# A two-layer cross-attention kernel: order of the opening's work and loads, the wait places of the weights, and filler matmuls on an idle TensorE

## The chip, the cores and the metric

The kernel runs on one core of a Trainium2 chip. The metric is the device time of one execution in microseconds (us), lower is better. Before the change the median of three runs is 1741.35 us (1740.72 to 1744.32).

## The reference

Two layers of grouped-query cross-attention are applied one after the other to `x` (32 batches, 112 rows, 512 features). The context (32 x 375 x 512) and an additive mask (32 x 112 x 375, all zeros in these inputs, but read and honoured) are the same for both layers; each layer has its own weights. Everything is float32. Per layer:

```
q = x @ Wq + bq           # 32 heads of 16, in 8 groups of 4
k = ctx @ Wk + bk         # 8 key heads of 16
v = ctx @ Wv + bv
scores = q . k / 4 + mask                     # 32 batches, 32 heads, 112 x 375
out = softmax(scores) @ v                     # over the 375
x = layernorm(out @ Wo + bo + x) * gamma + beta
```

## The kernel before

**Units and slots.** A unit is one batch of one layer. Units have a parity p (0 or 1) and a number n, batch 2n+p of layer 0 for n below PER = 16, of layer 1 above. The program is a row of slots (p, i), i from -1 to 33, p = 0 and then 1 in each i. Every engine runs its own program over the same slots, and they meet by semaphores alone. In slot (p, i) (function `units`) the work of several units lies side by side: the scores, exponentials and first half of the weighted values of the main unit (p, i); the row maxima and the values' projection of the unit ahead (1-p, i+p); the second half of weighted values and the first output heads of the unit behind; the projection of keys of unit (p, i+1) and, in slots of parity 0, of the queries of both parities; the last heads, the residual and the layer norm of the unit stored. A slot has 12 pieces; tables (`STEPS_AT`, `KEYS_AT`, `VALUES_AT`, `QUERIES_AT`, `COLUMNS_AT`, ...) say which work goes into which piece. `table_row(p, i)` picks the row: 0 or 1 by parity, and 2 for the slot (1, -1).

**Exact scores on bfloat16.** Queries and keys are split into three bfloat16 parts each (ScalarE casts and GpSimd subtracts), and small DMAs stack six products of parts along the contraction, 12 DMAs for each half of the heads of a unit: `stack_terms` on SyncE's queue (SP), `send` on ScalarE's (ACT) in the opening. The row maxima come first: 14 steps a unit, in each of which TensorE fills a pair of PSUM banks (L1090) and VectorE reduces it (L922); the step n+2 waits until the reduce n is done. Once a half's maxima are done, GpSimd splits them (L603 to L609), TensorE turns them (`max_columns`, L1122), ScalarE copies them (`mT`, L759), and one DMA (`max_rows`, L411) puts them as three more rows under the queries of the main unit. `scores` waits for it at pieces 0 and 6. The exponentials (L740) then need no more subtraction.

**The opening.** SyncE issues, in this order: Wk, context (0,0), Wq, the queries' input of both parities, context (1,0), Wv, and five of seven parts of the mask's bits. ScalarE's queue has issued the other two parts of the bits before anything else (`BEARLY = 2`). VectorE reduces each part of the bits to a column (L898) and all to one flag (L900 to L904); from it TensorE picks a program with or without the mask's addition. Ahead of that, TensorE runs the projections of slots (0, -1) and (1, -1): keys (0,0), the queries, keys (1,0), values (0,0). After the flag, slot (1, -1) has only the maxima of unit (0,0), and then (0, 0) starts, the first full slot.

**Weights.** In the opening slot (1, -1) SyncE issues `max_rows(0, 0, 1)` after the keys' stack, and then Wo and the rows bo, gamma, beta of layer 0. `next_layer`, called at the end of SyncE's slot, issues layer 1's Wk, bk, Wv, bv and three rows at (0, 0), half of Wq at (1, 0), the rest at (0, 1), half of Wo at (1, 1), the rest at (0, 14). TensorE, VectorE and GpSimd wait for all of layer 0's (`w_in[0]`) at the start of slot (1, 0), and for all 12 of layer 1's (`w_in[1]`) at the start of (0, 15). SyncE's queue is in program order: what is issued late for one unit makes all behind it late.

Of the kernel before, what the change touches and what calls it, by code (L numbers as in the profile page):

```python
# [15 lines left out]
NG = NH // NKV  # L16
LAYERS = 2
PAR = 2
# [29 lines left out]

BEARLY = 2
# [20 lines left out]


LATE_HEADS_AT = [{}, {0: (2,), 1: (3,)}]
HEADS_AT = [{10: (0,), 11: (1,)}, {8: (0,), 9: (1,), 10: (2,), 11: (3,)}]
KEYS_AT = [{2: (0,), 3: (1, 2), 4: (3,)}, {2: (0, 1), 3: (2, 3)}, {0: (0, 1, 2, 3)}]
VALUES_AT = [{1: (0, 1), 2: (2,)}, {4: (0,), 5: (1,), 6: (2,)}, {0: (0, 1, 2)}]
# [5 lines left out]
QUERY_PARTS_AT = [7, 5, 1]  # L81
QUERY_REST_AT = [9, 6, 2]
SEND_QUERIES_AT = 3
# [5 lines left out]
OUT_AT = [(11, 1), (9, 1)]  # L89
KEYS_END = [max(at) for at in KEYS_AT]  # L90
# [3 lines left out]
def step_order(q):  # L94

    order, whole, n = [], 0, 0
    for k in range(PIECES):
        first = min(STEPS_AT[q][k], (k not in WORK_FIRST[q]) + (k in WORK_LAST[q]))
        here = []
        for part, count in ((0, first), (1, k in MIXED_AT[q]), (2, STEPS_AT[q][k] - first)):  # L100
            for _ in range(count):
                half, tiles = (0 if k == 0 else 1, (MIXED, MIXED + TILES // 2)) if part == 1 else \
# [9 lines left out]
ORDER = [step_order(q) for q in range(PAR + 1)]  # L112
# [33 lines left out]
def table_row(p, i):  # L146

    return 2 if first_values(p, i) else p
# [7 lines left out]
def first_outputs(p, i):  # L156

    return isinstance(i, int) and (p, i) == (1, 0)
# [28 lines left out]
def cross_attention_two_layers(nc, xT_d, x_d, ctxT_d, mask_d, mflat_d, W, out):  # L187
# [4 lines left out]
    with ExitStack() as ctx:  # L192
# [96 lines left out]
        w_in = two(sem, "w_in")  # L289
        mf_in = [sem(f"mf_in{n}") for n in range(BLOADS)]  # L290
# [53 lines left out]
        NK, NQ, NV, NW = 2, 2, 2, (4, 12)  # L344
# [4 lines left out]
        def _(sp):  # L349
# [105 lines left out]
            def slot(p, i, has, lay):  # L455
# [28 lines left out]
                if m_ok:  # L484
                    load_x(p, main, lay[0])
                if j_ok:
# [17 lines left out]
                if isinstance(i, int):  # L504
                    next_layer(p, i)
# [26 lines left out]
            ROWS = [(bo, "bo"), (gamma, "gamma"), (beta, "beta")]  # L532

            def load_rows(L, landed):
                for dst, key in ROWS:
                    load_row(dst, L, key, landed)

            def next_layer(p, i):

                if (p, i) == (0, 0):  # L540
                    load_wk(1, w_in[1])
                    load_wv(1, w_in[1])
                    load_rows(1, w_in[1])
                if (p, i) == (1, 0):
                    load_wq(1, w_in[1], slice(0, 2))
                if (p, i) == (0, 1):
                    load_wq(1, w_in[1], slice(2, DC))
                if (p, i) == (1, 1):
                    load_wo(1, w_in[1], slice(0, 2))
                if (p, i) == (0, PER - 2):  # L550
                    load_wo(1, w_in[1], slice(2, NG))
# [6 lines left out]
            load_ctx(1, 0, 0)  # L558
            load_wv(0, w_v)
            for n in range(BEARLY, BLOADS):  # L560
# [8 lines left out]
        def _(pool):  # L569
# [5 lines left out]
            nc.gpsimd.memset(ks[1][:, :, :], 1.0).then_inc(ids, 1)  # L575
            nc.gpsimd.memset(vs[1][:, :, :, :, 1], 1.0).then_inc(ids, 1)
            pool.wait_ge(ids, 7)
# [7 lines left out]
            nc.gpsimd.memset(neghalf[:, :], -0.5).then_inc(ones_set, 1)  # L585

            def slot(p, i, has, lay):
# [4 lines left out]
                if first_outputs(p, i):  # L592
                    pool.wait_ge(w_in[0], 16 * NW[0])
# [32 lines left out]
                def key_parts():  # L626
                    pool.wait_ge(k_p1[p], proj + 1)
                    nc.gpsimd.tensor_tensor(kr[:, :], kf[:, :], kp[p][:, 0, :], ALU.subtract).then_inc(k_r[p], 1)  # L628
                    pool.wait_ge(k_p2[p], proj + 1)
                    nc.gpsimd.tensor_tensor(kp[p][:, 2, :], kr[:, :], kp[p][:, 1, :], ALU.subtract).then_inc(k_p3[p], 1)  # L630

# [18 lines left out]
                def residual_rows():  # L650
                    pool.wait_ge(x_in[o], 16 * (post + 1))
# [24 lines left out]
                elif first_values(p, i):  # L676
                    key_parts()
                    query_rests()
                    query_parts()
                    max_parts(o, 0, ahead, None)  # L680
                elif p == 0:
# [38 lines left out]
        def _(act):  # L720
            def slot(p, i, has, lay):
# [85 lines left out]
                if opens(p, i) and p == 0:  # L807
# [32 lines left out]
                for k in range(PIECES):  # L840
# [31 lines left out]
                    if opens(p, i) and k == SEND_QUERIES_AT:  # L872
                        act.wait_ge(q_p1[p], 2)
                        act.wait_ge(q_p2[p], 2)
                        act.wait_ge(q_p3[p], 2)
                        send(0, qs[p], qp, 0, range(PARTS))
# [10 lines left out]
        def _(dve):  # L887
# [18 lines left out]
            def slot(p, i, has, lay):  # L906
# [4 lines left out]
                if first_values(p, i):  # L911
                    dve.wait_ge(w_v, 16 * NV)
                if first_outputs(p, i):
                    dve.wait_ge(w_in[0], 16 * NW[0])
# [9 lines left out]
                def values():  # L924
                    dve.wait_ge(v_ps[o], ahead + 1)
# [31 lines left out]
                def centred():  # L957
# [381 lines left out]
```

## Time and profile before

| | |
|---|---|
| median of three runs | 1741.35 us |
| the profiled execution | 1738.81 us |
| its span, first to last instruction | 1737.0 us |
| TensorE busy | 1695.1 us, 98% |
| VectorE, ScalarE, GpSimd busy | 73%, 60%, 33% |
| mean granted TensorE clock | 0.99 |

PE is TensorE's matmul, PEld its weight load, DVE VectorE, ACT ScalarE, POOL GpSimd, SPq and ACTq the issue of DMAs on SyncE's and ScalarE's queues. Times are us from the first instruction. A clock of 1.00 is 2.4 GHz and 0.50 is 1.2 GHz; a window that has both shows a mean. Ahead of the first clock record of an execution the view shows 1.00 whatever the clock was. A float32 matmul of the program is two instructions in the trace. Sizes in KB are of 1024 bytes. In the view of sums a row has the window in us, its length, the busy us and the count of instructions (x) of PE, PEld, DVE, ACT and POOL, the mean granted clock, the DMA engines' share and GB/s. In the views in time order a row has start, us, engine, line, operation, operands and count, and in brackets the idle time before it and what ended it.

### The profile page before, as it was taken

The numbers are of one execution on the slowest core, as the hardware profiler recorded it, in microseconds if no ns is written. First come the engines' busy times: TensorE is split into PE (matmuls) and PEld (weight loads), VectorE is DVE, ScalarE is ACT, GpSimd is POOL, SyncE is SP. The second block draws the span as 40 slices with busy tenths as digits, with TensorE's granted clock in tenths as the row PEclk, the third lists the DMA queues.
The fourth block names the chain that finished last, engine by engine and source line by source line (L and its number), as shares of the span: only waits on it lengthen the run. The fifth ranks groups of instructions, "written<-read, shape, count | busy, mean of one in ns | idle before, by whom it ended". The sixth has DMA issues, their size and how long they took to land. (4 is left out here: it accounts for less than half of the span.)

```text
span 1737.0 us, 35992 instructions
## 1 busy us (share of the span) xinstructions
PE 1695.1 (98%) x10881; PEld 1005.9 (58%) x10881; DVE 1267.2 (73%) x1713; ACT 1042.3 (60%) x2370; POOL 572.3 (33%) x1169
## 2 busy tenths in 40 slices
PE   5999999999999999999999999999999999999997
PEld 3555566665565665565665565655665655656652
DVE  5567777787777777777777776777767877767776
ACT  2556666666665656665656665666656666656564
POOL 3133332333332333332333323333323333323332
PEclk8899999999999999999999999999999999999999
DMA  8546555455545465555565454455454455453541
GB/s 283 146 121 170 147 122 143 128 145 143 147 120 142 124 151 145 135 130 147 128 156 145 114 136 130 118 135 145 105 135 125 128 138 139 109 135 115 139 113 55
DMA packets 288390, 235.83 MB, mean 136 GB/s; under 512 B 140858, under 2 KB 262964, under 8 KB 288084
## 3 DMA queue, kind: packets, MB, share of 16 engines
q1 hardware_dynamic: 266852, 204.14, 43.8%
q10 hardware_dynamic: 21488, 31.06, 7.3%
q8 instruction: 27, 0.44, 0.1%
q14 instruction: 23, 0.19, 0.0%
HBM read 101.39 MB, written 22.02 MB: 71 GB/s over the span
## 5 line engine op out<-in xcount | busy, mean ns | idle before, releaser
L922 DVE TENSOR_REDUCE mx<-ms 128x2 f32<-128x750 f32 x896 | 809.2, 924 | 399.0 <-PE ms L1090 392.5
L740 ACT ACTIVATE probs<-sc 125x448 f32<-125x448 f32 x1522 | 744.6, 542 | 281.8 <-PE sc L1061 274.7
L1090 PE MATMUL ms<-ks,qs 96*128 96x375 bf16 (+1 forms) x2560 | 443.0, 327 | 11.4 <-DVE mx L922 8.7
L1061 PE MATMUL sc<-qs,ks 99*125 99x448 bf16 x1522 | 429.2, 358 | 6.0 <-DMA qs<-mT 3.7
L1111 PE MATMUL pv<-probs,vs 125*32 125x448 f32 x3048 | 313.2, 544 | 0.0
L1061 PEld LDWEIGHTS sc<-qs,ks 99*125 99x125 bf16 x1522 | 192.7, 137 | 204.2 <-ACT probs L740 127.8
L1090 PEld LDWEIGHTS ms<-ks,qs 96*128 96x128 bf16 (+1 forms) x2560 | 174.8, 98 | 194.3 <-issue 66.2
L1165 PE MATMUL job<-wo,on 128*112 128x512 f32 x504 | 258.2, 594 | 0.0
L936 DVE RECIPROCAL orec<-osum 128x112 f32<-128x112 f32 x256 | 213.0, 834 | 6.8 <-DMA osum<-oraw 6.8
L1183 PE MATMUL job<-xT,wq 128*128 128x224 f32 x1008 | 214.5, 356 | 0.0
L1134 PEld LDWEIGHTS job<-wv,ctxT 128*125 128x125 f32 x1536 | 191.5, 189 | 16.5 <-issue 0.3
L1148 PE MATMUL pv<-ctxT,wk 128*128 128x375 f32 x512 | 190.1, 484 | 10.7 <-DMA ctxT<-in_ctxT 10.7
L1183 PEld LDWEIGHTS job<-xT,wq 128*128 128x128 f32 x1008 | 187.4, 190 | 19.6 <-ACT qf L782 7.3
L1134 PE MATMUL job<-wv,ctxT 128*125 128x128 f32 x1536 | 196.0, 274 | 0.0
L1111 PEld LDWEIGHTS pv<-probs,vs 125*32 125x32 f32 x3048 | 86.1, 109 | 179.3 <-issue 171.7
L748 ACT COPY oraw<-pv 128x448 f32<-128x448 f32 x127 | 67.6, 532 | 200.1 <-PE pv L1111 200.1
L628 POOL TENSOR_TENSOR kr<-kf,kp 128x375 f32<-128x375 f32 x64 | 57.3, 895 | 357.7 <-ACT kp L771 357.7
L648 POOL TENSOR_TENSOR rstd<-veps,neghalf 112x1 f32<-112x1 f32 x64 | 36.4, 569 | 258.1 <-DVE veps L955 258.1
L1148 PEld LDWEIGHTS pv<-ctxT,wk 128*128 128x128 f32 x512 | 93.4, 192 | 47.0 <-issue 12.8
L617 POOL TENSOR_TENSOR on<-oc,orec 128x224 f32<-128x224 f32 x126 | 83.4, 662 | 86.3 <-DVE orec L936 85.7
L603 POOL TENSOR_TENSOR mwide<-mx,zero 128x14 bf16<-128x14 f32 x128 | 27.3, 213 | 241.9 <-DVE mx L922 234.5
L636 POOL TENSOR_TENSOR qr<-qf,qp 128x224 f32<-128x224 f32 x128 | 75.7, 613 | 69.0 <-ACT qp L796 69.0
(70 smaller groups left out, 1034.5 us busy)
## 6 DMA issues: line engine op xcount, KB each, us to landing
ctxT<-in_ctxT SPq DMA_DIRECT2D x64, 750.0 KB, 4.7
qs<-qp SPq DMA_DIRECT2D x756, 56.0 KB, 2.5
ks<-kp SPq DMA_DIRECT2D x765, 46.9 KB, 2.7
osum<-oraw ACTq DMA_DIRECT2D x125, 112.0 KB, 2.9
oc<-oraw ACTq DMA_DIRECT2D x125, 112.0 KB, 3.6
mask<-in_mask SPq DMA_DIRECT2D x64, 164.1 KB, 5.1
xT<-in_xT SPq DMA_DIRECT2D x32, 224.0 KB, 4.6
xin<-in_x SPq DMA_DIRECT2D x32, 224.0 KB, 3.0
```

Source lines behind the costliest of these rows:

```text
L617: nc.gpsimd.tensor_tensor(on[:, cols], oc[:, cols], orec[:, cols], ALU.mult).then_inc(on_ready[o], 1)
L636: nc.gpsimd.tensor_tensor(qr[:, cols], qf[:, p, cols], qp[:, 0, cols], ALU.subtract)\
L740: nc.scalar.activation(probs[0:KCS, k, j, :], bank[0:KCS, 0:GL], ACT.Exp)\
L922: nc.vector.tensor_reduce(mx[o][:, cols], ms[n % 2][:, :, 0:S2], AX_X, ALU.max).then_inc(max_done[o], 1)
L936: nc.vector.reciprocal(orec[:, S * n:S * n + S], osum[:, S * n:S * n + S])\
L1061: last = nc.tensor.matmul(bank[0:KCS, 0:GL], ks[p][0:KM, g, rows], qs[p][0:KM, g, :], start=True, stop=not masked)
L1090: last = nc.tensor.matmul(to, qs[o][0:KT, group, cols], ks[o][0:KT, group, :], start=True, stop=not masked)
L1111: last = nc.tensor.matmul(bank[32 * j:32 * j + 32, 0:GL], vs[u][:, chunk, 4 * h + j, :, :].rearrange("s d two -> s (d two)"), probs[0:KCS, ...
L1134: last = nc.tensor.matmul(job[0:KCS, P * c:P * c + P], ctxT[o][:, t, KCS * c:KCS * c + KCS], wv[lay[1]][:, t, :], start=(t == 0), stop=(t ...
L1148: last = nc.tensor.matmul(pv[:, 0:S2], wk[lay[3]][:, t, :], ctxT[p][:, t, :], start=(t == 0), stop=(t == DC - 1))
L1165: last = nc.tensor.matmul(bank[0:S, 0:D], weighted[:, S * c:S * c + S], wo[layer][:, c, :], start=(c == 0), stop=(c == NG - 1))
L1183: last = nc.tensor.matmul(bank[:, PAR * S * (c % 2):PAR * S * (c % 2 + 1)], wq[lay[3]][:, t, c, :], xT[:, t, :, :].rearrange("p u l -> p ( ...
```

## The change

It does five things. The mask's bits go all on SyncE's queue, ahead of context (1,0) and Wv, which now are issued inside the opening slot (0, -1), among the stacking DMAs. TensorE no longer runs slot (1, -1)'s projections ahead of the flag: keys (1,0) go into pieces 0 to 3 and values (0,0) into pieces 8 to 10 of slot (1, -1), after the flag, beside the maxima. Slot (0, 0) gets a table row of its own (row 3), with no maxima in pieces 0 and 1. TensorE runs 3 filler matmuls (float32, 112 x 448) before the keys and 12 between the queries and the flag. The loads of layer 0's Wo, bo, gamma, beta and of layer 1's weights are spread to the middle of slots, after `load_x`, and each wait for them is moved to the instruction that uses them. GpSimd's preparation of `ident` no longer waits for two memsets.

```diff
+CLOCK = (3, 12)
-KEYS_AT = [..., {0: (0, 1, 2, 3)}]
-VALUES_AT = [..., {0: (0, 1, 2)}]
+KEYS_AT = [..., {0: (0,), 1: (1,), 2: (2,), 3: (3,)}]
+VALUES_AT = [..., {8: (0,), 9: (1,), 10: (2,)}]
-QUERY_PARTS_AT = [7, 5, 1]
-QUERY_REST_AT = [9, 6, 2]
-SEND_QUERIES_AT = 3
+QUERY_PARTS_AT = [7, 5, 0]
+QUERY_REST_AT = [9, 6, 1]
+SEND_QUERIES_AT = (7, 7)
+for table in (STEPS_AT, KEYS_AT, VALUES_AT, COLUMNS_AT, MIXED_AT, QUERY_PARTS_AT, QUERY_REST_AT, WORK_FIRST, WORK_LAST):
+    table.append(table[0])
+STEPS_AT[3] = [0, 0, 2, 2, 1, 2, 1, 1, 0, 2, 0, 1]
+MIXED_AT[3] = (2, 8)
+KEYS_AT[3] = {3: (0,), 4: (1, 2), 5: (3,)}
...
+        NK, NQ, NV, NW, NR = 2, 2, 2, (3, 7), (2, 5)
...
             def opening_slot(p):
+                if p == 1:
+                    max_rows(0, 0, 1)
                 sp.wait_ge(k_p3[p], 1)
                 if p == 0:
                     stack_terms(0, 0, ks[0], kp[0], 1)
+                    stack_terms(0, 1, ks[0], kp[0], 1, of=(1, 2))
                     sp.wait_ge(q_p1[0], 2)
                     stack_terms(0, 0, qs[0], qp, 0, of=(0,))
-                    stack_terms(0, 1, ks[0], kp[0], 1, of=(1, 2))
+                    stack_terms(0, 1, ks[0], kp[0], 1, of=(0,))
+                    load_ctx(1, 0, 0)
+                    load_wv(0, w_v)
                     stack_terms(0, 1, qs[0], qp, 0, of=(0,))
                     load_mask(0, 0, 0)
                 else:
                     stack_terms(1, 0, ks[1], kp[1], 1)
                     load_ctx(0, 1, 0)
                     for u in range(PAR):
                         load_xT(u, 1, 0)
-                    max_rows(0, 0, 1)
-                    load_wo(0, w_in[0])
-                    load_rows(0, w_in[0])
+                    load_wo(0, w_in[0], slice(0, 2))
...
                 if m_ok:
                     load_x(p, main, lay[0])
+                if isinstance(i, int):
+                    weights(p, i)
                 if j_ok:
                     sp.wait_ge(k_p3[p], keys)
...
-                if isinstance(i, int):
-                    next_layer(p, i)
...
+            def weights(p, i):
+                if (p, i) == (0, 0):
+                    load_wo(0, w_in[0], slice(2, NG))
+                    load_row(bo, 0, "bo", w_in[0])
+                if (p, i) == (1, 0):
+                    load_row(gamma, 0, "gamma", rows_in[0])
+                    load_row(beta, 0, "beta", rows_in[0])
+                if (p, i) == (0, 1):
                     load_wk(1, w_in[1])
                     load_wv(1, w_in[1])
-                    load_rows(1, w_in[1])
-                if (p, i) == (1, 0):
+                if (p, i) == (1, 1):
                     load_wq(1, w_in[1], slice(0, 2))
-                if (p, i) == (0, 1):
+                if (p, i) == (0, PER - 2):
                     load_wq(1, w_in[1], slice(2, DC))
-                if (p, i) == (1, 1):
-                    load_wo(1, w_in[1], slice(0, 2))
-                if (p, i) == (0, PER - 2):
-                    load_wo(1, w_in[1], slice(2, NG))
+                if (p, i) == (1, PER - 2):
+                    load_wo(1, rows_in[1], slice(0, 2))
+                if (p, i) == (0, PER - 1):
+                    load_wo(1, rows_in[1], slice(2, NG))
+                if (p, i) == (1, PER - 1):
+                    for dst, key in ((bo, "bo"), (gamma, "gamma"), (beta, "beta")):
+                        load_row(dst, 1, key, rows_in[1])
             load_wk(0, w_k)
             load_ctx(0, 0, 0)
             load_wq(0, w_q)
             load_xT(0, 0, 0)
             load_xT(1, 0, 0)
-            load_ctx(1, 0, 0)
-            load_wv(0, w_v)
-            for n in range(BEARLY, BLOADS):
+            for n in range(BLOADS):
                 sp.dma_start(mbits[:, BROW * n:BROW * (n + 1)], mbits_d[n]).then_inc(mf_in[n], 16)
...
                 elif first_values(p, i):          # GpSimd, slot (1, -1)
-                    key_parts()
                     query_rests()
                     query_parts()
+                    key_rests()
                     max_parts(o, 0, ahead, None)
+                    key_lasts()
...
-                    act.wait_ge(k_p3[0], 1)       # ScalarE, slot (0, -1)
-                    act.wait_ge(ones_set, PAR)
-                    send(1, ks[0], kp[0], 1, (0,))
...
-            for n in range(BEARLY):
-                act.dma_start(mbits[:, BROW * n:BROW * (n + 1)], mbits_d[n]).then_inc(mf_in[n], 16)
...
+            def keep_clock(times):
+                for _ in range(times):
+                    nc.tensor.matmul(ms[0][0:S, 0, 0:GL], ident4[:, 0, :], ident4[:, :, :].rearrange("p c l -> p (c l)"),
+                                     start=True, stop=True)
+            keep_clock(CLOCK[0])
             pe.wait_ge(w_k, 16 * NK)
-            for p in range(PAR):
-                slots(False, opening=True)(p, -1, exists(p, -1), layers(p, -1))
-            pe.wait_ge(idd, 3)
+            slots(False)(*FIRST, exists(*FIRST), layers(*FIRST))
+            keep_clock(CLOCK[1])
             pe.wait_ge(flag_col, BLOADS + 1)
```

## Rows read from the trace of the kernel before

**Rows 1.** The page, part 1: busy us, share of the span, instructions.
```profile
PE 1695.1 (98%) x10881; PEld 1005.9 (58%) x10881; DVE 1267.2 (73%) x1713; ACT 1042.3 (60%) x2370; POOL 572.3 (33%) x1169
```
**Rows 2.** Waits of TensorE, whole span: us in total, times, longest us.
```profile
PE pv L1148 <- DMA ctxT<-in_ctxT: 10.7, 1, 10.7
...
PE sc L1061 <- DMA qs<-mT: 3.7, 1, 3.7
```
**Rows 3.** Sums, one slot's first exponential to the next's: (0,0), (1,0), (1,1), (0,3), (1,3).
```profile
47.41:76.07 28.66, 27.86 (x163) 18.63 (x165) 13.83 (x16) 16.46 (x38) 5.95 (x15) 0.89 0.35 105
76.07:107.07 31.00, 26.22 (x155) 13.96 (x144) 16.41 (x19) 15.55 (x36) 8.21 (x18) 0.89 0.58 164
134.87:159.65 24.78, 24.78 (x158) 13.06 (x157) 19.22 (x27) 15.70 (x35) 8.61 (x18) 1.00 0.66 170
212.38:240.31 27.93, 27.75 (x184) 18.20 (x184) 20.42 (x27) 16.96 (x39) 9.06 (x19) 1.00 0.45 126
240.31:264.88 24.57, 24.57 (x159) 13.15 (x159) 19.25 (x27) 15.52 (x35) 8.60 (x18) 1.00 0.71 164
```
**Rows 4.** TensorE in time order, 231 to 242 us, in slot (0, 3).
```profile
232.71 2.46 PE L1111 MATMUL pv<-probs,vs 125*32 125x448 f32 x24
...
237.25 1.02 PE L1165 MATMUL job<-wo,on 128*112 128x512 f32 x2
238.11 0.63 PE L1061 MATMUL sc<-qs,ks 99*125 99x448 bf16 x2
```
**Rows 5.** SyncE's queue in time order, slot (1, 0) and the like slot (1, 1).
```profile
75.73 0.42 SPq L515 DMA_DIRECT2D wk<-in_Wk  x1
...
79.11 0.62 SPq L365 DMA_DIRECT2D mask<-in_mask  x1
...
90.06 0.78 SPq L411 DMA_DIRECT2D qs<-mT  x1
...
135.58 1.81 SPq L365 DMA_DIRECT2D mask<-in_mask  x1
...
145.05 0.76 SPq L411 DMA_DIRECT2D qs<-mT  x1
```
**Rows 6.** TensorE and VectorE in time order, the opening.
```profile
10.65 5.34 PE L1148 MATMUL pv<-ctxT,wk 128*128 128x375 f32 x8 [10.65 <-DMA ctxT<-in_ctxT]
15.79 3.38 PE L1183 MATMUL job<-xT,wq 128*128 128x224 f32 x16
22.04 2.69 PE L1148 MATMUL pv<-ctxT,wk 128*128 128x375 f32 x8
24.57 2.78 PE L1134 MATMUL job<-wv,ctxT 128*125 128x128 f32 x24
29.36 1.72 DVE L898 TENSOR_REDUCE mcols<-probs 128x1 f32<-128x1500 uint32 x1 [2.16 <-DMA probs<-in_mask_bits]
31.41 0.37 PE L1261 MATMUL sc<-ident,mcol 128*1 128x128 f32 x1 [4.07 <-DVE mcol L900]
33.64 1.56 PE L1090 MATMUL ms<-ks,qs 96*128 96x375 bf16 x10 [1.85 <-DMA qs<-qp]
35.88 11.05 DVE L922 TENSOR_REDUCE mx<-ms 128x2 f32<-128x750 f32 x12
```
**Rows 7.** Sums of the opening's stretches, columns as in rows 3.
```profile
0.00:10.65 10.65, 0.00 (x0) 0.03 (x1) 3.96 (x5) 1.49 (x2) 5.19 (x15) 1.00 0.75 282
27.35:33.64 6.29, 0.37 (x1) 0.08 (x2) 2.30 (x4) 1.58 (x3) 1.79 (x2) 0.70 1.10 187
33.64:46.80 13.16, 11.03 (x42) 2.24 (x42) 11.92 (x14) 1.67 (x5) 3.15 (x8) 0.50 0.61 166
```
**Rows 8.** DMA issues over the span: count, KB each, median us to landing.
```profile
ctxT<-in_ctxT SPq DMA_DIRECT2D x64, 750.0 KB, 4.7
probs<-in_mask_bits ACTq DMA_DIRECT2D x2, 750.0 KB, 7.0
wk<-in_Wk SPq DMA_DIRECT2D x2, 256.0 KB, 4.7
```

More of the change, by code:

```diff
@@ L47 @@
 BLOADS = 7
-BEARLY = 2
 BROW = B * S * S2 // (BLOADS * P)
@@ L101, in step_order @@
             for _ in range(count):
-                half, tiles = (0 if k == 0 else 1, (MIXED, MIXED + TILES // 2)) if part == 1 else \
+                half, tiles = (MIXED_AT[q].index(k), (MIXED, MIXED + TILES // 2)) if part == 1 else \
                     (whole // len(WHOLE), WHOLE[whole % len(WHOLE)])
@@ L109, in step_order @@
     return order
-ORDER = [step_order(q) for q in range(PAR + 1)]
+ORDER = [step_order(q) for q in range(len(STEPS_AT))]
 OPENS = [[min(n for at in o for n, h, _, _ in at if h == half) for half in range(2)] for o in ORDER]
@@ L146, in table_row @@
 def table_row(p, i):
-    return 2 if first_values(p, i) else p
+    return 2 if first_values(p, i) else 3 if isinstance(i, int) and (p, i) == (0, 0) else p
 def opens(p, i):
@@ L156, in first_outputs, with first_rows @@
 def first_outputs(p, i):
-    return isinstance(i, int) and (p, i) == (1, 0)
+    return isinstance(i, int) and (p, i) in ((1, 0), (1, PER))
+def first_rows(p, i):
+    return isinstance(i, int) and (p, i) == (0, 1)
 def last_scores(p, i):
@@ L289, in cross_attention_two_layers @@
         w_in = two(sem, "w_in")
+        rows_in = two(sem, "rows_in")
         mf_in = [sem(f"mf_in{n}") for n in range(BLOADS)]
@@ L650, in residual_rows @@
                 def residual_rows():
+                    if first_outputs(p, i) and i == 0:
+                        pool.wait_ge(w_in[0], 16 * NW[0])
+                    if first_outputs(p, i) and i == PER:
+                        pool.wait_ge(rows_in[1], 16 * NR[1])
                     pool.wait_ge(x_in[o], 16 * (post + 1))
@@ L676, in slot @@
                 elif first_values(p, i):
-                    key_parts()
                     query_rests()
                     query_parts()
+                    key_rests()
                     max_parts(o, 0, ahead, None)
+                    key_lasts()
                 elif p == 0:
@@ L871, in slot @@
                             cast_rests(h)
-                    if opens(p, i) and k == SEND_QUERIES_AT:
+                    if opens(p, i) and k == SEND_QUERIES_AT[0]:
                         act.wait_ge(q_p1[p], 2)
+                        send(0, qs[p], qp, 0, (0,))
+                    if opens(p, i) and k == SEND_QUERIES_AT[1]:
                         act.wait_ge(q_p2[p], 2)
                         act.wait_ge(q_p3[p], 2)
-                        send(0, qs[p], qp, 0, range(PARTS))
-            for n in range(BEARLY):
-                act.dma_start(mbits[:, BROW * n:BROW * (n + 1)], mbits_d[n]).then_inc(mf_in[n], 16)
+                        send(0, qs[p], qp, 0, (1, 2))
             act.wait_ge(warm_set, 1)
@@ L1016, in slot @@
                             reciprocal(k - RECIPROCALS_AT[p])
+                if first_outputs(p, i) and i == PER:
+                    dve.wait_ge(rows_in[1], 16 * NR[1])
             run(dve, slot)
@@ L1022, in _, with slots @@
         def _(pe):
-            def slots(masked, opening=False):
+            def slots(masked):
                 def slot(p, i, has, lay):
@@ L1037, in slot @@
                     job_free = [(o_evac[p], stored + 1) if s_ok else (mt_evac[p], 2 * main + 1) if m_ok else None]
-                    if first_values(p, i):
-                        job_free[0] = (q_evac, NG // 2) if opening else (v_ready[o], 1)
+                    if isinstance(i, int) and (p, i) == (0, 0):
+                        job_free[0] = (v_ready[p], 1)
                     def take_job_bank():
@@ L1129, in project_values @@
                             take_job_bank()
-                        if first_values(p, i):
+                        if 0 in chunks and first_values(p, i):
                             pe.wait_ge(w_v, 16 * NV)
@@ L1163, in project_outputs @@
                             pe.wait_ge(on_ready[u], 2 * n + heads[0] // 2 + 1)
+                        if 0 in heads:
+                            if first_outputs(p, i) and i == 0:
+                                pe.wait_ge(w_in[0], 16 * NW[0])
+                            if first_outputs(p, i) and i == PER:
+                                pe.wait_ge(rows_in[1], 16 * NR[1])
                         for c in heads:
@@ L1217, in maxima @@
                         def maxima(part):
-                            for n, half, tiles, place in ORDER[q][k] if a_ok and not opening else ():
+                            for n, half, tiles, place in ORDER[q][k] if a_ok else ():
                                 if place == part:
                                     maximum(n, half, tiles, place)
-                        if k == 0 and a_ok and masked and not opening:
+                        if k == 0 and a_ok and masked:
                             pe.wait_ge(mask_in[o], 16 * (ahead + 1))
-                        if k == PIECES - 1 and a_ok and not masked and not opening:
+                        if k == PIECES - 1 and a_ok and not masked:
                             pe.wait_ge(mask_in[o], 16 * (ahead + 1))
@@ L1246, in slot @@
                             maxima(1)
-                        if k == COLUMNS_AT[q][0] and a_ok and not opening:
+                        if k == COLUMNS_AT[q][0] and a_ok:
                             max_columns(o, 0, ahead)
```

45 lines of the change are left out of this document (17 added, 28 removed).

## Prediction

> **What bounds the kernel.** I read the page's busy shares first: TensorE is busy for 98% of the span [rows 1], and no other engine comes above 73%. So only three things can move the time: TensorE's idle time, stretches at the low clock, and the work given to it. The list of TensorE's waits says where it idles. Two of its large entries are single waits: 10.7 us for the first context, and 3.7 us for a row of maxima [rows 2]. The sums by slot say where else time goes. In the steady state a pair of slots takes 27.93 + 24.57 = 52.50 us at clock 1.00. The first pair takes 28.66 + 31.00 = 59.66 us at a mean clock of 0.89 in both [rows 3], although it has less to do.
>
> How much less: slot (0, 0) has no unit behind it, so it lacks one half of weighted values (24 instructions, 2.46 us) and two output heads, each 0.86 us from its start to the start of what follows; slot (1, 0) lacks two heads [rows 4]. That is 2.5 + 1.7 + 1.7 = 5.9 us. The first pair's warm need is 52.5 - 5.9 = 46.6 us, and it has 59.66 - 46.6 = 13.1 us too much. Of these the clock explains (1 - 0.89) x 59.66 = 6.6 us (at half clock two us do the work of one, and the mean clock is the share of work done), the wait for the row of maxima 3.7 us, and the rest, 2.8 us, is smaller waits and idle time of slot (1, 0), where TensorE was busy for 26.22 of 31.00 us.
>
> **The change part by part.**
>
> *Loads spread, waits where they are used.* In slot (1, 0) SyncE begins with seven loads of layer 1 between 75.73 and 79.11 us, then issues the mask, 12 stacking DMAs and the row of maxima at 90.06. That row is what scores wait for at piece 6. From mask to row it takes 10.95 us there, and 9.47 us in slot (1, 1) [rows 5]. So the row is late by 3.4 us of issue and 1.5 us of slower issue behind full queues, together 4.9 us, which is more than the wait of 3.7 us. The change takes all seven loads out of this place. What is put into slot (1, 0) instead, gamma and beta, comes behind the row and `load_x`. The wait goes. What is late next is TensorE's own work, as in slot (1, 3), which is 24.57 us busy of 24.57. The low clock behind the wait goes with it. In slot (0, 0) SyncE gets half of Wo and bo ahead of the next keys' stack: two issues, about 1 us, beside TensorE's full work; if its cover is gone it costs that 1 us. In slot (0, 1) four loads, in (1, 1) one, and two, one, one and three around the layers' border come at the same place. Parity 1 has the tighter queue (9.47 us of issue without a pause), so its three row loads in (1, 15), some 1.3 us, could show; slot (1, 1) took 24.78 us with loads beside it, 0.21 above (1, 3) [rows 3]. I take 0 for all of them, between -0.5 and +2. The moved waits themselves guard loads issued a slot or more ahead: 0. In the case that one holds, what is queued behind it is TensorE's output heads, and the norm behind them.
>
> *Slot (0, 0)'s low clock.* TensorE ran the opening slot at 0.50 [rows 7], because it had nothing in it but maxima in step with VectorE's reduces (12 reduces in 11.05 us, 0.92 each [rows 6]), and took this clock into slot (0, 0). After the change the opening slot holds the dense projections of keys and values, so I expect the clock high at its end. Gain in the pair by both parts: 13.1 us. Against it stands the new table row of slot (0, 0): no maxima in pieces 0 and 1, then three steps in piece 2. VectorE needs 0.92 us for each, TensorE less, so it waits for one or two reduces: 1 us (0 to 2). The pair then takes 47.6 us: **-12.1 us**.
>
> *The flag.* Its last part of the bits is read at 29.36 us, and TensorE has the column at 31.41 [rows 6]. Ahead of this part before stood context (1,0) (750 KB) and Wv with its row (256 + 62 KB, Wv as large as Wk) [rows 8], 1.09 MB, which now come later. The loads ran at 282 GB/s up to 10.65 us and near 400 later; at 0.4 MB/us that is 2.7 us. The flag's matmul comes at 28.7 us. The bounds are 0 (the stacking DMAs of ScalarE's queue, now 4 us earlier, share the engines with the last bits) and -4.
>
> *The first context.* 2 x 750 KB of bits were issued ahead of everything on ScalarE's queue and shared the engines with it. Without them it lands sooner, by 0 to 4 us (1.54 MB at 0.4 MB/us); I take 2.5 us, so keys start at 8.2 us.
>
> *Filler matmuls.* The trace has none. The nearest row is the keys' float32 matmul of 375 columns: 8 instructions in 5.34 us at first, 2.69 us later [rows 6]. For 448 columns that is 0.40 us an instruction at the fast pace and 0.80 us at the slow. Three fillers are 6 instructions, 2.4 to 4.8 us, and are over before 8.2 us if `ident4` is ready by 3.4 us, which GpSimd's shorter preparation allows (its 15 instructions took 5.19 us before [rows 7]). Cost 0; they may save up to 2.7 us of the keys. The queries' input was there by 15.79 at the latest; 2.5 us sooner is 13.3, and 32 instructions (15.79 to 22.04, 6.25 us) end at 19 to 19.6 us. The 12 fillers, 24 instructions, then take 9.6 us, to about 29 us. That is level with the flag at 28.7: cost 0 to 0.5 us. At the slow pace they would take 19.2 us (a rival below).
>
> *The opening slot.* From flag to first maxima 2.23 us passed, and a queries' stack ended that wait [rows 6]; now 28.9 + 2.2 = 31.1 us. Before, the slot took 13.16 us, set by VectorE [rows 7]. Now keys (1,0) stand in piece 0 behind two maxima, and wait for context (1,0). Its issue is behind 12 stacking DMAs, and its data behind the bits. About 18 such DMAs of 50 KB (0.9 MB) at 187 GB/s, the rate of 27.35 to 33.64 us [rows 7], take 4.8 us from the last bits at 26.6, and then 0.77 MB at 0.4 MB/us 1.9 us: 33.3 us. All later maxima are queued behind this wait on TensorE, so VectorE, GpSimd's split and the row of maxima are late by it: about 1.4 us, between 0 and 4. Values (0,0) in pieces 8 to 10 are 24 instructions in 2.78 us, 0.93 a chunk [rows 6], and a step of maxima costs TensorE 11.03 / 14 = 0.79 us at half clock, so 0.4 to 0.5 at full. Such a piece has 1.4 us of TensorE against 0.92 of VectorE: 3 x 0.5 = 1.5 us. The keys' chunks, 0.67 us, hide. Slot: 13.2 + 1.4 + 1.5 = 16.1 us, end at 47.2 us against 46.8: **+0.4 us**, between -4 and +5. So the opening gives nothing for itself: what the flag wins is spent on projections that before ran in the shadow of the wait for it.
>
> *Removed from ScalarE and GpSimd.* Three stacking DMAs change queue and `key_lasts` comes later; both lie beside VectorE's maxima: 0.
>
> **Sum.** -12.1 + 0.4 = -11.7 us. From the profiled execution's 1738.81 us (span 1737.0 and 1.8 around it) this makes 1727.1 us. The median of the three runs is 2.54 us above the profiled one, so the forecast for the median is 1729.6 us.
>
> **A rule weighed against it.** The opening slot's row shows clock 0.50 for a TensorE that is busy for 11.03 of 13.16 us [rows 7]; it had idled 5.9 us of the 6.3 us before. The Trainium skill, "TensorE: Matmul & The Clock Gate", in "HAM oscillation — how this bites in real kernels", says that waits for DMAs between bursts of matmuls bring the array back to its low clock, burst after burst. By it fillers that end 2 us ahead of the maxima, and a wait for a context right behind those, leave the slot low again, and the time would be that of the first rival, 1734; by the row alone, which has a longer pause, it stays open. The trace agrees as far as the fall goes: it shows it behind two pauses, of 4.07 and of 3.73 us.
>
> **Rivals.**
> (a) *The clock falls in the opening slot, and returns with the dense pieces.* For: pauses of 2.2 and 1.4 us follow each other with little between them, and both pauses of 4 us in this trace were followed by 0.50. Against: they are shorter. Price: keys and the maxima among them at half clock, 4 chunks x 0.67 and 4 pairs x 0.3 us, some 3.9 us, and half a us more later: 1729.6 + 4.4 = 1734.
> (b) *The moved loads keep part of the wait.* For: no pause in parity 1's queue. Against: slot (1, 1) had loads and took only 24.78 us. Price: the 3.7 us stall shrinks to half, and smaller ones of 1 us come in (0, 1), (1, 1) and (1, 15), 1.9 + 2 = 3.9 us: 1733.5.
> (c) *The opening wins too.* If the context (1,0) is there in time and bits land 4 us sooner, the slot's end moves from 47.2 to 43.2: 1725.6.
> (d) *Slower: the long fillers run at the slow pace.* If the clock isn't up when they start, they take 19.2 us, the queries 12.5 and the keys 5.3: 8.2 + 5.3 + 12.5 + 19.2 = 45.2 us, and the flag's matmul waits for them, 16.3 us behind the forecast's 28.9. 1729.6 + 16.3 = 1745.9. It decides from the point where the fillers end over 28.9 + 11.7 = 40.6 us. Against it: the queries and second keys ran at the fast pace 5 us behind the first keys [rows 6].
> (e) *The change doesn't do what it says:* the pair's excess has another cause, say DMA traffic of the contexts, and stays: 1740 to 1742.
>
> **How the numbers follow.** Chances: forecast 0.52, (a) 0.17, (b) 0.10, (c) 0.14, (d) 0.04, (e) 0.03. The forecast's own range is 1727 to 1733. For 8 in 10 it has to reach towards (a) and (c), and takes in the opening's bounds of -4 and +4: 1724.5 to 1736. A measurement of this kernel can't tell less than 0.2%, 3.5 us, from no change, so faster means below 1737.9 and slower above 1744.8. (d) is slower; (e) and a tenth of (a) and (b) are within: faster 0.90, same 0.06, slower 0.04.
>
> **What would show it.** The slot sums: first pair at 47 to 49 us from its first exponential to that of (0, 1), clock 1.00. TensorE's waits: none for qs<-mT at L1061, and a new one of 1 to 2 us for the context at L1148 in slot (1, -1). The first exponential at 46 to 49 us. Keys' first 8 instructions under 4 us. Steady pairs at 52.4 to 52.6 us as before. The forecast is wrong if the clock is 0.50 beyond 40 us, if the flag's matmul comes right behind a filler well after 29 us, or if the pair still takes over 52 us.

## The result and the profile after

The changed kernel takes 1729.24 us (median of 4 runs, 1728.31 to 1732.09) against 1741.77 for the kernel before (4 runs): ratio 0.9929, 95% interval 0.9911 to 0.9946. The forecast was 1729.6. Run twice more, on the chips of the experiments, it stood at 0.9949 (0.9933 to 0.9965) and 0.9949 (0.9933 to 0.9966), so by the medians the gain is 8.6 to 12.5 us.

The profiled execution is 1728.31 us, span 1726.5: 10.5 us below that of before. The page, part 1:

```profile
PE 1695.4 (98%) x10911; PEld 1007.9 (58%) x10911; DVE 1266.7 (73%) x1713; ACT 1041.5 (60%) x2370; POOL 572.2 (33%) x1169
```

TensorE's busy time is that of [rows 1], but 13.4 us of it are now the fillers (30 instructions). The program's own 10881 instructions take some 13 us less than before: 5.8 in the opening, 5.5 in the first pair, 1.7 behind it. Of the first pair's 8.1 us below, 5.5 are less busy time and 2.6 less idle time; what the opening's own work saves stands there as idle time or fillers.

The waits of TensorE over the whole span, against [rows 2]: the wait for qs<-mT is gone. Where 10.7 us stood for the first context, the fillers' wait for their operand stands (3.1 us), and the keys wait 2.0 us in the opening slot for context (1,0), which is new.

```profile
PE ms L1112 <- DVE mx L940: 9.3, 39, 1.1
PE pv L1168 <- DMA ctxT<-in_ctxT: 3.3, 3, 2.0
PE ms L1283 <- POOL negident L597: 3.1, 1, 3.1
PE ms L1112 <- DMA qs<-qp: 2.8, 2, 2.6
PE sc L1083 <- ACT probs L765: 1.5, 4, 0.6
```

Sums from one slot's first exponential to the next's, slots (0,0), (1,0), then a steady pair. The columns are those of [rows 3]:

```profile
46.97:74.87 27.90, 25.50 (x163) 16.57 (x166) 13.85 (x17) 16.46 (x38) 6.00 (x15) 1.00 0.55 158
74.87:98.52 23.65, 23.10 (x155) 12.41 (x144) 15.94 (x19) 15.67 (x35) 8.08 (x18) 1.00 0.76 168
...
256.34:284.19 27.85, 27.67 (x184) 18.20 (x183) 20.44 (x27) 16.95 (x39) 9.06 (x19) 1.00 0.42 115
284.19:308.76 24.57, 24.57 (x159) 13.16 (x159) 19.26 (x27) 15.51 (x35) 8.61 (x18) 1.00 0.71 163
```

The first pair went from 59.66 us to 27.90 + 23.65 = 51.55, both slots at clock 1.00, where 47.6 was forecast. Nearly all of that came in slot (1, 0), 31.00 to 23.65. The first exponential moved by 0.4 us, from 47.41 to 46.97. So 8.5 of the 10.5 us are had by 98.5 us, and 2.0 come later, in small pieces.

SyncE's queue in time order in slot (1, 0), against [rows 5]: the mask is the first issue behind the context, the row of maxima goes out 8.1 us later (10.95 before), and gamma and beta follow behind it.

```profile
73.95 0.53 SPq L373 DMA_DIRECT2D ctxT<-in_ctxT  x1
74.53 0.42 SPq L378 DMA_DIRECT2D mask<-in_mask  x1
74.99 3.74 SPq L419 DMA_DIRECT2D ks<-kp  x6
78.78 3.80 SPq L419 DMA_DIRECT2D qs<-qp  x6
82.61 0.78 SPq L424 DMA_DIRECT2D qs<-mT  x1
85.66 0.33 SPq L399 DMA_DIRECT2D xin<-in_x  x1
86.04 0.42 SPq L528 DMA_DIRECT2D gamma<-in_gamma  x1
```

TensorE in time order in the opening, against [rows 6] (L1283 the fillers, L1168 keys, L1208 queries, L1292 the flag, L1112 maxima):

```profile
3.08 4.23 PE L1283 MATMUL ms<-ident 112*112 112x448 f32 x6 [3.08 <-POOL negident L597]
7.38 2.77 PE L1168 MATMUL pv<-ctxT,wk 128*128 128x375 f32 x8
11.48 3.26 PE L1208 MATMUL job<-xT,wq 128*128 128x224 f32 x16 [1.34 <-DMA xT<-in_xT]
14.59 3.19 PE L1208 MATMUL sc<-xT,wq 128*128 128x224 f32 x16
17.61 9.19 PE L1283 MATMUL ms<-ident 112*112 112x448 f32 x24
26.90 0.27 PE L1292 MATMUL sc<-ident,mcol 128*1 128x128 f32 x1
29.76 1.02 PE L1112 MATMUL ms<-ks,qs 96*128 96x375 bf16 x10 [2.60 <-DMA qs<-qp]
32.82 1.62 PE L1168 MATMUL pv<-ctxT,wk 128*128 128x375 f32 x2 [2.04 <-DMA ctxT<-in_ctxT]
34.23 0.83 PE L1112 MATMUL ms<-ks,qs 96*128 96x375 bf16 x2
```

Keys start 3.3 us sooner and run at the fast pace (8 in 2.77 us, not 5.34). The long fillers end at 26.8 us and the flag's matmul comes at 26.9. But from 29.76 us a pair of maxima takes 0.83 us and a keys' chunk 1.62: the slow pace. The granted clock shows it in the sum of that slot, of the same kernel:

```profile
29.76:46.58 16.82, 13.24 (x74) 7.57 (x74) 11.71 (x14) 3.25 (x8) 4.90 (x10) 0.80 0.33 96
```

16.82 us, where 13.16 stood in [rows 7] and 16.1 was forecast. The clock fell to 0.50 at 30.5 us, between the two pauses of 2.6 and 2.0 us, and was back at 37.3 us.

### The profile page after: what moved, and what is told of

Its sections match the earlier page's. It is cut to its first block and busy times, and to the rows that moved or that the text cites. A ratio compares the mean times of both kernels' runs of the same rounds, so it can differ in the third digit from the quotient of the medians.

```text
span 1726.5 us, 36049 instructions
## 1 busy us (share of the span) xinstructions
PE 1695.4 (98%) x10911; PEld 1007.9 (58%) x10911; DVE 1266.7 (73%) x1713; ACT 1041.5 (60%) x2370; POOL 572.2 (33%) x1169
## 5 line engine op out<-in xcount | busy, mean ns | idle before, releaser
L1112 PE MATMUL ms<-ks,qs 96*128 96x375 bf16 (+1 forms) x2560 | 437.9, 324 | 12.4 <-DVE mx L940 9.3
L1112 PEld LDWEIGHTS ms<-ks,qs 96*128 96x128 bf16 (+1 forms) x2560 | 174.0, 98 | 190.8 <-issue 66.5
L1208 PE MATMUL job<-xT,wq 128*128 128x224 f32 x1008 | 214.3, 356 | 1.3 <-DMA xT<-in_xT 1.3
L1208 PEld LDWEIGHTS job<-xT,wq 128*128 128x128 f32 x1008 | 187.1, 190 | 20.9 <-ACT qf L807 7.1
L1168 PE MATMUL pv<-ctxT,wk 128*128 128x375 f32 x512 | 189.9, 482 | 3.5 <-DMA ctxT<-in_ctxT 3.3
L1168 PEld LDWEIGHTS pv<-ctxT,wk 128*128 128x128 f32 x512 | 93.0, 192 | 40.1 <-issue 3.6
```

Source lines behind the costliest of these rows:

```text
L1112: last = nc.tensor.matmul(to, qs[o][0:KT, group, cols], ks[o][0:KT, group, :], start=True, stop=not masked)
L1168: last = nc.tensor.matmul(pv[:, 0:S2], wk[lay[3]][:, t, :], ctxT[p][:, t, :], start=(t == 0), stop=(t == DC - 1))
L1208: last = nc.tensor.matmul(bank[:, PAR * S * (c % 2):PAR * S * (c % 2 + 1)], wq[lay[3]][:, t, c, :], xT[:, t, :, :].rearrange("p u l -> p ( ...
```

## Experiments

Twelve runs in three groups; each ratio is to the kernel before, run in the same group. Beside it stand the first exponential (E) and the first pair (P) of the profiled execution.

| run | ratio (95%) | E, us | P, us |
|---|---|---|---|
| loads_only | 0.9967 (0.9954 to 0.9980) | 47.55 | 52.11 |
| loads_back | 1.0009 (0.9993 to 1.0025) | 47.42 | 64.15 |
| row0 | 0.9957 (0.9940 to 0.9974) | 48.71 | 53.47 |
| no_fill | 0.9951 (0.9935 to 0.9967) | 49.33 | 51.23 |
| after_again | 0.9949 (0.9933 to 0.9965) | 50.17 | 51.43 |
| pad_heads | 0.9961 (0.9948 to 0.9973) | 47.81 | 52.19 |
| bridge_ctx | 0.9967 (0.9951 to 0.9984) | 49.54 | 51.21 |
| fill_24 | 0.9976 (0.9963 to 0.9989) | 52.39 | 54.30 |
| loads_fill | 0.9948 (0.9932 to 0.9965) | 47.97 | 51.41 |
| fill_first | 0.9957 (0.9940 to 0.9973) | 49.31 | 51.29 |
| bits_act | 0.9934 (0.9917 to 0.9950) | 48.20 | 51.08 |
| after_third | 0.9949 (0.9933 to 0.9966) | 50.14 | 51.04 |

**The loads, alone and put back.** `loads_only` is the kernel before with the loads in the places of the change and each wait at the instruction that uses them; the cut shows the call alone. `loads_back` is the changed kernel with the loads back at the ends of the slots and in the opening slot, while the waits stay where they are used.

```diff
-                if isinstance(i, int):
-                    next_layer(p, i)      # at the end of SyncE's slot
                 if m_ok:
                     load_x(p, main, lay[0])
+                if isinstance(i, int):
+                    weights(p, i)
```

> The kernel before with nothing but the loads and their waits moved as in the change (opening as it was, no filler matmuls). My theory: the wait of 3.7 us for the row of maxima in slot (1, 0) came from SyncE's seven loads at its start, so it goes, with the low clock behind it and the 0.9 us for exponentials held up behind ScalarE's slow DMA issue; slot (0, 0) keeps its low clock. First pair 59.7 -> 53 to 54 us, total 6 to 7 us below the kernel before. Rival (the loads' traffic comes back in the middle of slots): pair 56 to 57 us and slots (0, 1), (1, 1) each 0.5 us longer, total 2 to 3 us below. Rival (the opening's order made the wait): pair within 1 us of before.

> The changed kernel with the loads put back at the ends of slots and in the opening, as before; waits stay where they are used. Theory: the wait for the row of maxima in slot (1, 0) returns at 3 to 4 us and the clock falls behind it, first pair 51.6 -> 57 to 58 us, total 6 to 7 us above the changed kernel. Rival (the new opening alone removes it): pair within 1 us of 51.6.

Slots (0,0) and (1,0) of loads_only:

```profile
47.55:76.37 28.82, 28.02 (x159) 18.73 (x161) 13.84 (x16) 16.45 (x38) 5.79 (x14) 0.88 0.26 85
76.37:99.66 23.29, 23.13 (x155) 12.52 (x148) 15.94 (x19) 15.58 (x35) 8.27 (x18) 1.00 0.73 174
```

The move alone takes 7.5 of the pair's 8.1 us, 0.9 us more than the most expected, all in slot (1, 0); slot (0, 0) keeps its low clock. Both rivals of loads_only fall. In loads_back the waits of TensorE from 47 to 112 us are:

```profile
PE sc L1080 <- DMA qs<-mT: 3.9, 1, 3.9
PE ms L1109 <- DMA qs<-qp: 3.3, 1, 3.3
```

The 3.9 us are the old wait, though the waits for the weights stand as in the change: it comes from where the loads are issued. How much of it is their place in the queue (3.4 us of issue) and how much their traffic (1.5 us of slower issue behind them) no run separates. The 3.3 us are new, and weren't expected: with Wo and the rows in front, SyncE issues the queries' stack of unit (1,0) at 57.5 to 61.3 us, when the maxima of slot (0, 0) already want it. So in the new opening the spread of loads is worth 64.15 - 51.55 = 12.6 us, more than in the old, and more than expected (5.4 to 6.4): reordered opening and spread loads aren't additive, and the opening with the old loads is no faster than the kernel before.

**Row 3.**

```diff
-    return 2 if first_values(p, i) else 3 if isinstance(i, int) and (p, i) == (0, 0) else p
+    return 2 if first_values(p, i) else p
```

> The changed kernel with slot (0, 0) on the table row 0 of the other slots, so maxima in pieces 0 and 1 again. Theory: the first step waits for the stack of unit (1, 0), whose last DMAs are issued at 47.4 us, some 3 us behind the slot's start, so TensorE idles 2 to 3 us in piece 0 and gets back about 1.3 us of the waits that row 3 has at pieces 2 to 6: pair 52 to 54 us, total +0.5 to +2. Rival (row 3 is what costs the pair its missing gain): pair 50 us, total -1.5.

As expected: TensorE waits 2.58 us behind the first scores for a stack of keys, and the pair is 53.47.

```profile
48.32 0.54 PE L1083 MATMUL sc<-qs,ks 99*125 99x448 bf16 x2
51.45 0.93 PE L1112 MATMUL ms<-ks,qs 96*128 96x375 bf16 x10 [2.58 <-DMA ks<-kp]
```

That stack, of unit (1, 0), is issued 11 us later in the new opening. Before, then in the changed kernel, where it stands behind the row of maxima:

```profile
32.33 3.74 SPq L406 DMA_DIRECT2D ks<-kp  x6
...
43.57 3.83 SPq L419 DMA_DIRECT2D ks<-kp  x6
```

**The pair's missing 4 us.** The dummies are put where the heads would be (`keep_clock` takes the bank as an argument here):

```diff
+                        if isinstance(i, int) and ((p, i) == (1, 0) and k in (0, 1) or (p, i) == (0, 0) and k in (10, 11)):
+                            take_job_bank()
+                            keep_clock(1, job)
```

> The changed kernel with one dummy float32 matmul of 448 columns (0.76 us) in each of the four places where slots (0, 0) and (1, 0) lack an output head: pieces 10 and 11 of the one, 0 and 1 of the other. The first pair was forecast at 47.6 us and took 51.6. Theory (TensorE waits there for ScalarE's two exponentials a piece, 1.08 us, so work that is missing there was never saved): 3.05 us of dummies cost 1.0 to 1.8 us, pair 52.6 to 53.4. Rival (TensorE is the bound in these pieces, as the prediction had it, and the missing 4 us are elsewhere): +3.0 us, pair 54.6.

Four dummies of 0.76 us make the pair 52.19, against 51.55, 51.43 and 51.04 in three executions of the changed kernel: 0.6 to 1.2 us for 3.05 us of work, at or below the low end of the theory. The two in slot (0, 0) cost nothing (27.89 us against 27.90), the two in slot (1, 0) cost it all (24.30 against 23.65, 23.53 and 23.14). The changed kernel first, then pad_heads (job<-ident at L1286), TensorE in time order around the slots' border:

```profile
71.41 0.54 PE L1083 MATMUL sc<-qs,ks 99*125 99x448 bf16 x2
72.54 0.74 PE L1083 MATMUL sc<-qs,ks 99*125 99x448 bf16 x2 [0.59 <-ACT probs L765]
73.12 0.48 PE L1112 MATMUL ms<-ks,qs 96*128 96x375 bf16 x2
73.64 0.74 PE L1083 MATMUL sc<-qs,ks 99*125 99x448 bf16 x2
74.32 2.46 PE L1133 MATMUL pv<-probs,vs 125*32 125x448 f32 x24
```

```profile
72.25 0.54 PE L1083 MATMUL sc<-qs,ks 99*125 99x448 bf16 x2
72.63 0.92 PE L1286 MATMUL job<-ident 112*112 112x448 f32 x2
73.38 0.74 PE L1083 MATMUL sc<-qs,ks 99*125 99x448 bf16 x2
```

Without a head, scores follow scores 1.13 and 1.10 us apart, which is the pace of ScalarE's two exponentials (0.54 us each); with the dummy they are 1.13 us apart too. At this border the dummy lies in the wait. So the four heads, 3.4 us in the prediction, were worth about 1 us, which explains some 2.4 of the missing 4 us. The absent half of weighted values (2.5 us) wasn't tested this way.

**The fillers.**

```diff
-CLOCK = (3, 12)
+CLOCK = (0, 0)      # no_fill;  (3, 0) fill_first;  (3, 24) fill_24
```

> The changed kernel without filler matmuls. Theory: the first keys take 5.3 us instead of 2.8, so the queries' parts and stacks come about 3 us later; the flag doesn't. TensorE is idle from about 20 to 27 us and the clock is low from there through most of slot (1, -1), whose 12.7 us of dense work raises it again before (0, 0). First exponential at 49 to 51 us instead of 47.0, total +2 to +4 us. Rival (fillers are worth nothing, the flag and the context set the opening): first exponential within 0.5 us of 47.0. Rival (the clock stays low into (0, 0)): +6 to +8 us.

> The changed kernel with the 3 fillers in front of the keys and none in front of the flag. Theory: the keys stay at 2.8 us and the stacks are on time, but TensorE idles from 17.6 to 26.9 us, and the clock is low at the first maxima and through the keys' chunks until dense work has run: 1 us or so over the changed kernel (without any filler it was at 49.3 us for the first exponential against 47.0 and 50.2 in two executions of the changed kernel). Rival (the long fillers are what the opening needs): as without any filler, +3 us. Rival (they only cost): 0 to -1.

> The changed kernel with 24 instead of 12 long fillers in front of the flag. Theory: the 12 end at 26.8 us, level with the flag's column at 26.9, so 12 more (9.2 us) come one for one on top, less what the stacks' wait of 2.6 us and the context's of 2.0 us take up: first exponential at 51.5 to 52.5 us, total +4.5 to +5.5. Rival (every us of filler delays the flag and nothing hides): +9.2 us.

Both kernels without long fillers have E at 49.3 us; the changed kernel has 46.97, 50.17 and 50.14. Three other runs have the same TensorE program up to E: loads_back, pad_heads and row0 (47.42, 47.81, 48.71). So by E nothing is shown for the fillers, and the intervals of no_fill, fill_first and the changed kernel overlap. From the first maxima to E it took 16.7 to 18.5 us in these six and 18.4 and 19.0 without the long fillers, so 1 or 2 us are possible, but two executions don't show them. In no_fill the keys took 4.70 us and TensorE then idled 9.35 us in front of the flag, and still the first maxima came at 30.97 us. fill_24 is as expected: the fillers hold the flag's matmul to 36.07 us, E is 52.4, the median 5.4 us above that of after_again. The flag is 9.2 us later than in the changed kernel's first execution and E 5.4, so 3.8 us are hidden: the wait for context (1,0) is gone, and a pause of 1.55 us is left in front of the maxima, where 2.60 stood. That its slot (1, 0) took 26.4 us, with 1.5 us of wait for a context and a low clock behind, wasn't foreseen.

**Bridging the gaps, and an earlier context.**

```diff
             with pe.If(any_mask == 0):
+                keep_clock(2)
                 run(pe, slots(False), after=FIRST)
...
+                            if first_values(p, i):
+                                pe.wait_ge(k_evac[o], 1)
+                                keep_clock(2, pv)
                             pe.wait_ge(ctx_in[p], 16 * (proj + 1))
...
+                    load_ctx(1, 0, 0)
                     stack_terms(0, 1, ks[0], kp[0], 1, of=(0,))
-                    load_ctx(1, 0, 0)
```

> The changed kernel with two fillers behind the flag's read and two in front of the wait for context (1,0), and this context issued three stacking DMAs earlier. Theory: the context lands 1 to 2 us sooner (the wait of 2.04 us shrinks below 1), and the clock doesn't fall at 30.5 us, so the keys' chunks in slot (1, -1) take 0.8 us each and not 1.6: first exponential at 45 to 46 us, total -1 to -2 us against the changed kernel. Rival (the wait is set by the bits and stacks ahead in the rings, and VectorE sets the slot): first exponential within 0.5 us of 47.0. Rival (fillers in front of the maxima delay them): 47.5 to 48.5.

A miss. TensorE from 27 us:

```profile
28.90 2.52 PE L1286 MATMUL ms<-ident 112*112 112x448 f32 x4 [1.56 <-issue]
31.21 1.58 PE L1112 MATMUL ms<-ks,qs 96*128 96x375 bf16 x10
32.73 3.33 PE L1286 MATMUL pv<-ident 112*112 112x448 f32 x4
35.85 1.16 PE L1171 MATMUL pv<-ctxT,wk 128*128 128x375 f32 x2
```

The clock fell all the same, four filler instructions then took 3.33 us instead of 1.5, and they, not the context, held the keys to 35.85 us. From the first maxima to these keys it takes 4.6 us, against 2.8 to 3.4 in the three executions of the changed kernel. So here the fillers in front of something that was nearly there cost some 1.5 us of that stretch; E (49.54) and the ratio don't tell it from the changed kernel's.

**The old opening with fillers.** loads_only, and in it:

```diff
+            keep_clock(2)
             pe.wait_ge(w_k, 16 * NK)
             for p in range(PAR):
                 slots(False, opening=True)(p, -1, exists(p, -1), layers(p, -1))
-            pe.wait_ge(idd, 3)
+            keep_clock(8)
             pe.wait_ge(flag_col, BLOADS + 1)
```

> The kernel before with the loads moved as in the change, its own opening kept (both contexts projected ahead of the flag, two parts of the bits on ScalarE's queue), and filler matmuls in the two places where TensorE idled: 2 in front of the keys, 8 in front of the flag. Theory: the first keys take 2.8 us instead of 5.3, the stacks come 2.5 us sooner and the wait of 1.9 us in front of the first maxima shrinks; the maxima set slot (1, -1) at 13.2 us as before, and the clock falls in it: first exponential at 46 us, pair 52 us, total within 1.5 us of the changed kernel without its reordered opening. Rival (the clock stays up through the maxima): pair 51 us, total 2 us below the changed kernel. Rival (the flag's bits set all): first exponential at 47.5 us.

The ratio equals the changed kernel's in both of its reruns, as expected, so the rearranged opening gives nothing that can be measured over the old. The way differs: the keys were not faster (4.88 us), E came at 47.97, not 46, and the pair at 51.41. Its slot (0, 0) stands on row 0, has its stacks in time, and 4.4 us at the low clock:

```profile
47.97:75.46 27.49, 26.69 (x159) 17.59 (x161) 13.82 (x16) 16.45 (x39) 5.80 (x14) 0.92 0.27 88
```

That is less than the 27.90 us of the changed kernel's slot on row 3 with no low clock. loads_only has 7.2 us of low clock in this slot and 28.82 us: 2.8 us less of it are worth 1.3 us. By the same rate a slot on row 0 with its stacks in time and no low clock would take some 25.3 us (an estimate), and row 3 with the late stack costs 2.6 us (an estimate), not the 1 us of the prediction. That is what the new opening gives back.

**Bits on ScalarE's queue.**

```diff
-            for n in range(BLOADS):
+            for n in range(2, BLOADS):     # SyncE; the first two on ScalarE's queue
```

> The changed kernel with two of the seven parts of the mask's bits on ScalarE's queue again, ahead of all. Theory: they share the DMA engines with Wk and the first context, so keys start at 10 to 11 us and not at 7.4, the stacks come 3 us later, and the bits, whose bytes are the same, end at the same time: flag at 26.9, first maxima at 31 to 32 us instead of 29.8, first exponential +1 to +2 us. Rival (DMA time is shared so that nothing but the flag counts): within 0.5 us.

> The changed kernel a third time, as a base on this group's chip and to see how far its opening varies: the first exponential stood at 46.97 us in one execution and 50.17 in the other. Theory (the bits' landing varies with the DMA engines, here and not in the kernel before, where it was 47.4 and 47.6): between 47 and 50.5 us; 8 to 12.5 us below the kernel before.

In bits_act keys start at 10.92 us, as expected, and the last part of the bits is read at 24.64 us. Here the fillers, which end at 30.4, hold the flag, 3.7 us behind its column; yet E is 48.2, between the changed kernel's three. The last part of the bits is read in the three executions of the changed kernel at 24.93, 27.98 and 26.41 us:

```profile
24.93 1.72 DVE L920 TENSOR_REDUCE mcols<-probs 128x1 f32<-128x1500 uint32 x1 [0.92 <-DMA probs<-in_mask_bits]
```

```profile
27.98 1.72 DVE L920 TENSOR_REDUCE mcols<-probs 128x1 f32<-128x1500 uint32 x1 [2.44 <-DMA probs<-in_mask_bits]
```

These are the first and the second execution. With it the first maxima move (29.76, 33.40, 31.66), and E by 3.2 us, though not one for one: the third execution has its maxima 1.7 us ahead of the second's and the same E. In both reruns the low clock of the opening slot lasted 10.2 us, to 40.4 and 41.4 us, in the first 6.8. Against 47.4 and 47.6 of before and loads_only, the new opening stands between -0.4 and +2.8 us.

bits_act has the lowest of the group's ratios, 0.9934, but its interval overlaps the changed kernel's 0.9949. With 6 long fillers in place of 12 it might beat both; that wasn't tried.

## Why the prediction was right

- *TensorE is the bound; its idle time and low clock in the opening and first pair are what can be won.* Right: 8.5 of 10.5 us went there, mostly as less busy time at the full clock.
- *Seven loads make the row of maxima late; the wait goes with its low clock.* Right, shown from both sides by loads_only and loads_back. What was late next in slot (1, 0) was TensorE's own work, as forecast: busy for 23.10 of 23.65 us.
- *Pair -12.1 us.* The term that was mis-sized: it measured -8.1 (-8.2 and -8.6 in the reruns). Two of its parts fail. First, "the first pair's warm need is 46.6 us" took the absent heads off the steady pair one for one, 3.4 us; pad_heads shows that 3.05 us there cost about 0.9. In slot (0, 0) they cost nothing, because scores follow the two exponentials, 1.1 us a piece; why the two heads of slot (1, 0) were worth only 0.7 to 1.2 us stays open. That is some 2.4 us too much. Second, row 3.
- *Row 3: 1 us (0 to 2).* TensorE waits 0.45, 0.80 and 0.34 us, 1.6 together, which is within the bounds; but by the lengths of slot (0, 0) in loads_only and loads_fill the late stack and row 3 cost 2.6 us (the estimate above), 1.6 more than forecast. With the 2.4 this makes the missing 4.0. row0 is worse still. On this reading the absent values were worth their 2.5 us, and "the clock explains 6.6 us" was fair for slot (0, 0); no run has row 0, its stacks in time and the full clock, so this division stays an estimate.
- *Flag at 28.7, first keys at 8.2, fillers 0.40 us an instruction, first maxima at 31.1, context at 33.3, slot 16.1 us.* Measured 26.9 (28.4 and 30.0 in the reruns), 7.4, 0.38, 29.8 (31.7, 33.4), 32.8, 16.8. All are near; the flag of the first execution came 4.5 us sooner than before, beyond its bound of 4.
- *Opening +0.4 us.* -0.4 in the first profile, +2.8 and +2.7 in the reruns. The centre was right by two errors that cancel in the first: bits 1.8 us sooner, and a low clock that the sum didn't have.
- *Rival (a), the clock falls in the opening slot and returns with the dense pieces* came true in every execution of the changed kernel, with pauses of 2.6 and 2.0 us in the first. The rule weighed in the prediction (the Trainium skill, "TensorE: Matmul & The Clock Gate", "HAM oscillation — how this bites in real kernels") fits the fall; the price of 4.4 us was not seen as a whole. In the first execution the two slowest keys' chunks (1.62 and 1.46 us) cost 1.5 us more than at the fast pace, VectorE was busy for 11.71 of the slot's 16.82 us, and E came as forecast. In the reruns the low clock lasted beyond 40 us, which the prediction had named as a sign that it is wrong, and E came at 50.1 and 50.2, outside the 46 to 49 that it gave. Their gain of 8.6 us is nearer to this rival's 7.3 than to the forecast's 11.7.
- *Moved loads cost 0 later:* the pair behind, (0, 1) and (1, 1), took 52.38 us against 52.58, and (1, 14) 25.78 against 25.11. Within the bounds, but contexts now come late at times: TensorE waits 0.4 us for one in (1, 0) and 0.9 us in (1, 14), where before had no such wait, 1.3 us there in loads_only, and 2.0 us in the second pair of no_fill, which took 54.56 us.
- *-11.7 us in all* against -10.5 by the profiles: -8.1 - 0.4, and -2.0 from the steady part and the end. These last were not forecast. The pairs of layer 2 took 52.43 us against 52.51, 0.9 us over the layer, also in the reruns (576.8 against 577.6 us for 22 slots), and not in loads_only (577.5) or loads_fill (577.6); its cause stays open.

So the direction, the place and the main mechanism were right; that the number fell within 0.4 us of the first median is partly luck. The profiled execution came 1.2 us above its forecast, and the median 0.9 us above that one, where 2.5 was assumed; and the reruns gained 8.6 us, not 12.5.

## What to carry to other kernels

Look at where in a queue's order a bulk load is issued, not only at whether there is time for it: seven loads of layer 1, wanted over 700 us later, cost 7.5 us with a 10 KB row behind them in the queue. A reordered opening must also deliver what the first full slot reads first: here a stack of keys that came 11 us later gave back some 2.6 us by estimate. When a bound engine has less to do in a stretch, don't take the missing work off its time one for one; ask at which pace the next engine lets it go on. And judge filler matmuls by a run without them: here their gain is below what 4 to 10 runs resolve, and in front of a nearly finished wait they held the work behind them.

## What the runs showed of the hardware

The same kernel's opening, which moves some 9 MB by 28 us in the first execution, small DMAs among them, ends anywhere within 3.2 us: in three executions the last 750 KB were read at 24.9, 26.4 and 28.0 us. TensorE's granted clock also fell near 1690 us, for 3.4 to 6.8 us, in seven of the fourteen profiled executions of all kernels (in none of before or of the changed one). From the first exponential of slot (0, 30) to the end these seven took 107.1 to 108.9 us, the others 105.4 to 106.4. Whoever compares two profiles to 1 us should look for both first.
